# Attention on one Trainium2 core: the output projection stands behind the first unit of the next block's body, and SyncE drops four implied signals

## The reference

```python
def _L0_attn_ref(x, w_qkv, w_proj, b_proj):        # x: layernorm of h, (128, 127, 192)
    ...
    q3, q4, q5 = (q[..., :g], q[..., g:2 * g], q[..., 2 * g:])
    k3, k4, k5 = (k[..., :g], k[..., g:2 * g], k[..., 2 * g:])
    v3, v4, v5 = (v[..., :g], v[..., g:2 * g], v[..., 2 * g:])
    x3 = merge(_attn(q4, jnp.concatenate([k3, k4], axis=2), jnp.concatenate([v3, v4], axis=2), scale))
    x4 = merge(_attn(q5, jnp.concatenate([k3, k5], axis=2), jnp.concatenate([v3, v5], axis=2), scale))
    x5 = merge(_attn(q5, jnp.concatenate([k4, k5], axis=2), jnp.concatenate([v4, v5], axis=2), scale))
    out = jnp.concatenate([x3, x4, x5], axis=2)
    return out @ w_proj.T + b_proj                 # h = h + this
```

## Time and profile before

| | before |
|---|---|
| median of three runs | 1845.01 us (1844.54 to 1849.14) |
| the profiled execution, its own time | 1846.4 us |
| its span in the trace | 1844.7 us |
| busy in the span: TensorE, VectorE, ScalarE, GpSimd | 1747.4, 1486.3, 1443.1, 1250.6 us |

### The profile page before, as it was taken

How to read it: one execution, slowest core, us unless ns; L and a number is a source line. 1 busy time by engine, 2 the same in 40 slices (tenths; PEclk the granted TensorE clock), 3 DMA queues, 4 the chain that set the end, 5 groups by cost and what they waited for, 6 DMA issues and landing times. The chain is left out here.

```text
span 1844.7 us, 56704 instructions
## 1 busy us (share of the span) xinstructions
PE 1747.4 (95%) x19008; PEld 1021.8 (55%) x19008; DVE 1486.3 (81%) x3546; ACT 1443.1 (78%) x2983; POOL 1250.6 (68%) x2306
## 2 busy tenths in 40 slices
PE   5999999599999999999999999999994999999999
PEld 3677777244444444444444444444442777777776
DVE  6887777689999999999999999999974555555554
ACT  4676676288899989899998989898984777777775
POOL 5677776467777777777777777777734656566661
PEclk9999999699999999999999999999997999999999
DMA  7344442144444444444444444444431332323232
GB/s 195 94 112 113 114 114 69 35 80 90 91 90 92 92 91 92 91 90 94 90 91 92 91 90 92 91 92 92 92 63 36 70 72 65 74 63 76 60 78 51
DMA packets 503935, 159.49 MB, mean 86 GB/s; under 512 B 452176, under 2 KB 503120, under 8 KB 503888
## 3 DMA queue, kind: packets, MB, share of 16 engines
q1 hardware_dynamic: 503888, 158.90, 40.7%
HBM read 37.26 MB, written 12.48 MB: 27 GB/s over the span
## 5 line engine op out<-in xcount | busy, mean ns | idle before, releaser
L757 DVE TENSOR_REDUCE tops<-p_maxa 128x6 f32<-128x762 f32 x512 | 483.1, 944 | 42.1 <-PE p_maxa L587 32.5
L664 PE MATMUL p_o<-probs,vn 127*32 127x256 f32 x6144 | 411.8, 386 | 0.3 <-DVE att L787 0.3
L707 ACT ACTIVATE probs<-p_s 128x512 f32<-128x512 f32 x512 | 305.2, 596 | 84.1 <-PE p_s L583 83.7
L583 PE MATMUL p_s<-qm,kt 32*128 32x256 f16 x3072 | 349.5, 273 | 4.1 <-DMA qm<-qk 1.1
L761 DVE TENSOR_REDUCE tops<-p_maxb 128x4 f32<-128x508 f32 x512 | 346.3, 676 | 0.0
L714 ACT ACTIVATE probs<-p_s 128x512 f32<-128x512 f32 x512 | 311.4, 608 | 2.2 <-PE p_s L583 2.2
L711 ACT ACTIVATE probs<-p_s 128x512 f32<-128x512 f32 x512 | 305.0, 596 | 0.0
L1066 DVE TENSOR_TENSOR gel_lo<-gel,gel_hi 128x512 f16<-128x512 f32 x192 | 150.8, 785 | 169.6 <-ACT gel_hi L1038 169.6
L583 PEld LDWEIGHTS p_s<-qm,kt 32*128 32x128 f16 x3072 | 135.4, 93 | 227.2 <-issue 126.7
L812 POOL TENSOR_TENSOR qk<-raw,one 128x384 f16<-128x384 f32 x128 | 105.7, 826 | 202.0 <-ACT raw L732 202.0
L664 PEld LDWEIGHTS p_o<-probs,vn 127*32 127x32 f32 x6144 | 160.8, 109 | 141.4 <-issue 75.5
(11 more groups left out here) (212 smaller groups left out, 4497.4 us busy)
## 6 DMA issues: line engine op xcount, KB each, us to landing
xt_a<-in_xt SPq DMA_DIRECT2D x32, 512.0 KB, 4.3
xt_b<-in_xt SPq DMA_DIRECT2D x64, 256.0 KB, 5.2
out<-out_sb SPq DMA_DIRECT2D x32, 336.0 KB, 2.6
xt<-hx SPq DMA_TRANSPOSE x128, 2.4
kt<-qk SPq DMA_TRANSPOSE x128, 2.8
qt<-qk SPq DMA_TRANSPOSE x128, 2.4
qm<-qk SPq DMA_TRANSPOSE x128, 2.7
yt<-ay SPq DMA_TRANSPOSE x128, 2.3
```

What stands on the lines that cost most here:

```text
L583: return nc.tensor.matmul(o, kt[full(j), r, kind, half, :], qm[full(j), r % 2, versions, half, :], start=True, stop=True, skip_group_check ...
L664: last = nc.tensor.matmul(p_o[32 * j:32 * j + 32, blocks, :], vn[0:NP, r, src:src + 32], probs[0:NP, r % 2, QUAD * g + j, kind * 256:(kind ...
L707: nc.scalar.activation(probs[:, r % 2, h + 1, 0:512], p_s[1][:, :, :].rearrange("p x n -> p (x n)"), ACT.Exp, scale=SCALE).then_inc(act_e1 ...
L757: nc.vector.tensor_reduce(top[:, q, 6 * pair:6 * pair + 6].rearrange("p (e k) -> p e k", e=2), p_ma[:, :, :].rearrange("p (e k) n -> p e k ...
```

## The change

The projection `proj(i)` moves on TensorE from behind unit 3 to behind unit 0 of the next body; since the body index then is one higher, it now works on block `i-3`. On VectorE the addition to `h` and the statistics change places. `z_reader` follows the new order. On SyncE three waits ahead of `kt` and one ahead of `qm` are left out, since what they wait for is implied by signals that are awaited anyway.

```diff
@@ SyncE, ahead of kt
-                    if within(i, NB):
-                        ready(pe_ma[1], seen(2 * (i + 1)))
-                        ready(pe_mb[1], seen(i + 1))
-                    if within(i - 2, NB):
-                        ready(pe_s0[3], seen(i - 1))
                     ready(pool_k, seen(i + 3))
@@ SyncE, ahead of qm
                     ready(dve_min, seen(i + 2))
-                    ready(pool_q5, seen(i + 2))
+                    if not within(i - 2, NB):
+                        ready(pool_q5, seen(i + 2))
@@ TensorE
-            def proj(i):
-                if within(i - 2, NB):
-                    pe.wait_ge(dma_y, seen(16 * (i - 1)))
-                    pe.wait_ge(*z_reader(i, 1))
+            def proj(i):
+                if within(i - 3, NB):
+                    pe.wait_ge(dma_y, seen(16 * (i - 2)))
+                    pe.wait_ge(*z_reader(i, 0))
                     rows(p_z[:, 0:C], yt, "wproj", t.bproj).then_inc(pe_proj, 1)
...
                 products(i, r, 0)
+                proj(i)
                 outputs(i - 1, before, 0, 2)
                 outputs(i - 1, before, 1, 0)
...
                 products(i, r, 3)
-                proj(i)
                 outputs(i, r, 0, 0)
                 outputs(i, r, 0, 1)
@@ VectorE
                 maxima(i, r, 0)
                 if within(i - 3, NB):
-                    dve.wait_ge(dve_h, seen(i - 2))
-                    nc.vector.bn_stats(...)
+                    b = i - 3
+                    dve.wait_ge(pe_proj, seen(b + 1))
+                    nc.vector.tensor_tensor(t.h[...], p_z[:, 0:C], t.h[...], ALU.add).then_inc(dve_h, 1)
...
                 maxima(i, r, 3)
-                if within(i - 2, NB):
-                    b = i - 2
-                    dve.wait_ge(pe_proj, seen(b + 1))
-                    nc.vector.tensor_tensor(t.h[...], p_z[:, 0:C], t.h[...], ALU.add).then_inc(dve_h, 1)
+                if within(i - 3, NB):
+                    dve.wait_ge(dve_h, seen(i - 2))
+                    nc.vector.bn_stats(...)
```

More of the change, by code:

```diff
@@ L561, in z_reader @@
                 i, use = (i, 0) if use else (i - 1, 1)
-                if use == 0 and within(i + 3, NB):
+                if use == 0 and within(i - 3, NB):
+                    return dve_h, i - 2
+                if use == 1 and within(i + 3, NB):
                     return act_v, i + 4
-                if use == 1 and within(i - 2, NB):
-                    return dve_h, i - 1
             return consts, 0
@@ L641, in qkv @@
                     pe.wait_ge(dma_x, seen(16 * (i + 4)))
-                    pe.wait_ge(*z_reader(i, 0))
+                    pe.wait_ge(*z_reader(i, 1))
                     rows(p_z[:, :], xt, "wqkv").then_inc(pe_qkv, 1)
             def proj(i):
-                if within(i - 2, NB):
-                    pe.wait_ge(dma_y, seen(16 * (i - 1)))
-                    pe.wait_ge(*z_reader(i, 1))
+                if within(i - 3, NB):
+                    pe.wait_ge(dma_y, seen(16 * (i - 2)))
+                    pe.wait_ge(*z_reader(i, 0))
                     rows(p_z[:, 0:C], yt, "wproj", t.bproj).then_inc(pe_proj, 1)
@@ L766, in body @@
                 if within(i - 3, NB):
-                    dve.wait_ge(dve_h, seen(i - 2))
-                    nc.vector.bn_stats(t.stats[:, bass.ds((i - 3) * 6, 6)], t.h[:, bass.ds((i - 3) * C, C)])
+                    b = i - 3
+                    dve.wait_ge(pe_proj, seen(b + 1))
+                    nc.vector.tensor_tensor(t.h[:, bass.ds(b * C, C)], p_z[:, 0:C], t.h[:, bass.ds(b * C, C)], ALU.add).then_inc(dve_h, 1)
                 maxima(i, r, 1)
@@ L790, in body @@
                 maxima(i, r, 3)
-                if within(i - 2, NB):
-                    b = i - 2
-                    dve.wait_ge(pe_proj, seen(b + 1))
-                    nc.vector.tensor_tensor(t.h[:, bass.ds(b * C, C)], p_z[:, 0:C], t.h[:, bass.ds(b * C, C)], ALU.add).then_inc(dve_h, 1)
+                if within(i - 3, NB):
+                    dve.wait_ge(dve_h, seen(i - 2))
+                    nc.vector.bn_stats(t.stats[:, bass.ds((i - 3) * 6, 6)], t.h[:, bass.ds((i - 3) * C, C)])
             loop(dve, body)
```

## The result

| | before | after |
|---|---|---|
| median, run side by side | 1844.78 us (1843.68 to 1849.14) | 1880.82 us (1877.56 to 1882.23) |
| ratio, 95% interval | | 1.0187 (1.0167 to 1.0207) |
| the profiled execution, its own time | 1846.4 us | 1877.56 us |
| busy: TensorE, VectorE, ScalarE, GpSimd | 1747.4, 1486.3, 1443.1, 1250.6 us | 1743.9, 1469.2, 1433.9, 1258.8 us |

The changed kernel is slower by 36.0 us by the medians, 31.2 by the two profiled executions. Forecast were 1892 us and a range of 1860 to 1901. TensorE, VectorE and ScalarE show a little less busy time in a longer run, and only GpSimd shows some more (8 us), so the loss is waiting.

A forecast was written before the change was run, and what follows sets the result against it. A ring of waits through TensorE and ScalarE bounds the kernel; bodies go from 7.76 to 8.28 us, 1.50 more a round, 45 over 30 rounds, about 47 in all: 1846.4 + 47 = 1893, forecast 1892 us, range 1860 to 1901.

The forecast's parts named there:

- Unit 0 barely gains: On TensorE, unit 0 would end 3.05 us behind the transposes, 0.07 earlier than before, held by VectorE's L761 of unit 3.
- The `p_maxb` wait of 0.73: Unit 0's p_maxb products would start 0.73 us behind L761's start, a delay read from unit 2 of the kernel before.
- The rival in which only `att` counts: p_maxb enters unit 0 without delay, only the outputs wait: body 8.00 to 8.09, 1856 to 1867 us; chance 10%.
- the main sum: The ring's terms for one body after the change: 4.64 + 3.64 = 8.28 us against 7.76.
- The projection behind unit 0 has no cover: On TensorE, unit 1 comes 0.59 us later relative to unit 0's end, 4.64 behind the transposes instead of 4.12.
- The clock: TensorE's clock stays at 1.00; as a rival, new waits drop it in one body in ten, 1996 us; chance 1%.
- the ring: Chain setting a body's length: transposes, unit 3, projection, outputs, units 0 and 1, three exponentials, unit 2's end, qkv; 7.76 us.
- then 0.48 to the five `qkv` matmuls: On TensorE, from unit 2's last scores, behind ScalarE's third exponential, to qkv: 0.48 us, taken as unchanged.
- 8.2 to 8.3 in all four bodies: Sign of being right: the period of GpSimd's L812 in every body of a round, in us.
- the 1 to 2 that I gave to the bodies outside the loop: Six or seven full bodies outside the loop, about 0.5 us each, give 3; 1 to 2 taken off for second digits.
- The signals: Four dropped SyncE signals cost at most 0.44 us, only in a round's first body, and bring nothing beside the move.
- faster: TensorE's own work without waits on the ring sets the body: 7.63 us, 1812 us in all; chance 6%.

The follow-up runs named there:

- e2_move_only: The changed kernel with the four SyncE waits put back, so only the projection and VectorE work are moved: 1881.03 us, 1.018 of the kernel before.
- e7_before_swap_vector: The kernel before with only the addition and the statistics exchanged on VectorE: 1844.63 us, 1.0005 of the kernel before.
- e3_move_short_max_unit3: The changed kernel with VectorE's L757 of unit 3 reading 16 of 127 columns: 1857.16 us, 1.0053 of the kernel before.
- its control: The kernel before with VectorE's L757 of unit 3 reading 16 of 127 columns: 1844.16 us, 1.0003 of the kernel before.
- e6_split_projection: The changed kernel with three of the projection's six matmuls back behind unit 3, three behind unit 0: 1848.55 us, 1.0023 of the kernel before.
- e9_move_short_exp_unit1: The changed kernel with ScalarE's third exponential of unit 1 making 64 of 512 columns: 1876.68 us, 1.0164 of the kernel before.
- e12_before_short_both_unit1: The kernel before with unit 1's third exponential cut to 64 of 512 columns and its p_maxb maximum to 16 of 127: 1833.67 us, 0.9941.
- e8_signals_loop_of_eight: The kernel before with the four SyncE waits dropped and eight bodies in the loop instead of four: 1949.18 us, 1.0579 of the kernel before.
- e1_signals_only: The kernel before with the four SyncE waits dropped and nothing moved: 1832.3 us, 0.992 of the kernel before.

## Why the prediction was right, and what in it was off

*The mechanism was right.* The loss is the projection's place (`e2_move_only`), not the signals and not VectorE's exchange (`e7_before_swap_vector`).

- *Unit 0 barely gains.* Said 3.05 behind the transposes; measured 3.06. `e3_move_short_max_unit3` against its control shows that L757 of unit 3 holds it, `e6_split_projection` that half the projection stands in the waits there for nothing.
- *The `p_maxb` wait of 0.73.* Measured 0.74 (835.43 to 836.17), and 0.73 in unit 2 of `e9_move_short_exp_unit1`. The size came out partly by luck, since the place it was read from doesn't show such a wait. There `p_maxb` stood 0.32 behind the start of unit 2 (832.58 to 832.90), and in `e12_before_short_both_unit1`, where this maximum ends early, it still does:

```profile
819.38 0.39 PE L583 MATMUL p_s<-qm,kt 32*128 32x256 f16 x4
...
819.70 0.38 PE L587 MATMUL p_maxb<-kt,qt 24*128 24x256 f16 x2
```

So it was TensorE's own work that gave the 0.73, and the row could only bound the wait from above.
- *The rival in which only `att` counts* is what `e3_move_short_max_unit3` makes: 1857.16, in its 1856 to 1867. Its 8.00 to 8.09 for the body were too high, like the main sum; measured 7.96.
- *The projection behind unit 0 has no cover.* Projection 0.60, outputs 1.00, unit 1 at 4.66 (4.64 said), ScalarE 0.44 behind.
- *The clock.* 1.00, with TensorE's new wait of 0.39 us in every body (the 0.38 and 0.71 are ScalarE's). Where the prediction has TensorE waiting up to 0.65 us at a time, show 0.26 idle behind 0.39 of scores. The rule of the Trainium skill, TensorE: Matmul & The Clock Gate, HAM oscillation, that waits repeated in a loop can lower the clock again and again, did not come in with waits of this length. Behind the standstills of some 3 us in `e8_signals_loop_of_eight` the clock did fall, as the last section shows.

*The term that was too large* is the last one but one of the ring, "then 0.48 to the five `qkv` matmuls". After the change it is 0.33 (840.16 to 840.49). I took the 0.48 of the earlier trace rows as what follows on ScalarE's third exponential. In the kernel before it was TensorE's own work: both `p_maxa` matmuls, the last scores and `p_maxb` stood behind the outputs together, and `e12_before_short_both_unit1` keeps that length (819.53 to 820.01). When unit 2 has to wait, `p_maxa` goes ahead (839.78), and only `p_maxb` is left behind the last scores. The sum becomes 3.06 + 0.60 + 1.00 + 0.44 + 1.63 + 0.33 + 1.09 = 8.15 instead of 8.28, so the sign "8.2 to 8.3 in all four bodies" held only for the one over the branch. A round is 32.66, not 33.12, and 30 x 0.46 = 14 us is most of the 16 between the 47 forecast and the 31.2 of the profiled executions; the 1 to 2 that I gave to the bodies outside the loop are the rest. By the medians the forecast was 11 us too high.

*The reading of the ring before* had a flaw that cost nothing. I read unit 1's L707 at 831.11 as following on unit 1's scores. ScalarE ran on without a break from unit 0's, and both ways give 831.11. The weight loads (PEld) of the kernel before show where TensorE waited for ScalarE's third exponential, in unit 1 and for unit 0's:

```profile
831.25 0.09 PEld L583 LDWEIGHTS p_s<-qm,kt 32*128 32x128 f16 x1 [0.30 <-ACT probs L714]
```

In unit 2 of the same body they show no wait for ScalarE. So the ring that was there went through the exponentials of unit 0 and the end of unit 1. This is read from the trace: no run shortened a reader of unit 0, and VectorE's maximum of unit 0 is as close (830.46 + 0.73 = 831.19). The ring that I described exists only after the change, and even then with a twin on VectorE that I didn't see: 839.36 + 0.73 = 840.09 against 840.16.

*The signals.* At most 0.44 us in a first body was the bound; they were worth 0.48. That they bring nothing beside the move holds for the medians. But the extra of the first body did not go under the ring wholly: 0.09 of it stayed (8.23 against 8.14).

*Not faster.* The rival "faster" was to be decided by unit 0's end at 2.53 behind the transposes. Not even with L757 cut did it get there (2.86). The part of the change that beats both kernels is the signals without the move, `e1_signals_only`.

## What to carry to other kernels

Before moving work from behind a wait to another place, ask whether it filled a wait there: a gap that closes on one engine may be held open by a second one with 0.1 us to spare, and then the work was partly free where it stood and may have no cover where it goes. Here 0.54 of the projection's 0.60 us arrived at unit 1 (4.66 against 4.12 behind the transposes), and 0.39 were left over the body, since a wait inside unit 1 went away. Take the length of a link from a place where the same thing holds it; a stretch that an engine fills with its own work gets shorter when that engine has to wait. And try the parts of a change apart: here one half alone gained some 14 us and the other alone lost 34 (1881.03 against 1847.05 beside it), and together they lost no less, so that the gain was hidden.

## What the hardware showed that I had not expected

With eight bodies in the loop instead of four, the program's code itself seems to go over the DMA queues: 113 instruction packets, 1.85 MB, in 900 us against 2 packets before, and once in a round TensorE stands with nothing to wait for but its issue, 2.65 to 3.39 us at a time. The steady stretch of that kernel has a granted clock of 0.97 instead of 1.00, and behind the standstill that ends at 818.32 it is 0.50:

```profile
400.00:1300.00 900.00, 823.13 (x10451) 388.68 (x10448) 778.29 (x1433) 738.86 (x1535) 616.98 (x1229) 0.97 0.52 84
818.30:822.00 3.70, 3.68 (x36) 1.29 (x36) 2.05 (x4) 1.75 (x4) 2.02 (x5) 0.50 0.79 117
```

There the sixteen matmuls of `outputs` take 1.94 us instead of 1.07. So part of the 117 us is the standstill, and part the matmuls behind it at the lower of the two clock levels (1.2 GHz): together they make the body with the standstill 13.49 (813.34 to 826.83) instead of some 7.8. A third part lies outside. The seven bodies ahead of it take 56.93 (756.41 to 813.34), 2.4 more than seven in `e1_signals_only`, and the clock of 760 to 800 us is 1.00; what holds them I have not settled. That the packets are the loop's code fetched anew in each round is an inference from their kind and number, with no run that varies the length in smaller steps.
